# A constant tile written ahead of each row scatter on GpSimd, in place of a lag by tiles

## What is computed

```
x = x + cross_attention_0(layernorm(x), context 77 keys, 16 heads)
x = x + ffn_0(layernorm(x))          # top-1 gate of 8, LoRA of rank 4, relu
x = x + cross_attention_1(layernorm(x), context)
x = x + moe_1(layernorm(x))          # top-1 switch of 8 experts, 128 -> 512 -> 128, gelu
```

```
out[t] = x[t] + p[t] * (gelu(xn[t] @ w1[e] + b1[e]) @ w2[e] + b2[e])
```

## Time and profile before

| | us |
|---|---|
| three runs | 205.21, 207.39, 207.83 |
| their median | 207.39 |
| the profiled execution, its own time | 206.03 |
| its span in the profile | 204.2 |
| TensorE busy | 172.5 (84%) |
| VectorE busy | 124.7 (61%) |
| ScalarE busy | 90.5 (44%) |
| GpSimd busy | 59.9 (29%) |
| 22 output scatters on GpSimd, together | 21.6 |
| 8 row scatters on GpSimd, together | 8.4 |

### The profile page before, as it was taken

How to read it: one execution, slowest core, us unless ns; L and a number is a source line. 1 busy time by engine, 2 the same in 40 slices (tenths; PEclk the granted TensorE clock), 3 DMA queues, 4 the chain that set the end, 5 groups by cost and what they waited for, 6 DMA issues and landing times.

```text
span 204.2 us, 3819 instructions
## 1 busy us (share of the span) xinstructions
PE 172.5 (84%) x1168; PEld 141.8 (69%) x1169; DVE 124.7 (61%) x386; ACT 90.5 (44%) x216; POOL 59.9 (29%) x73
## 2 busy tenths in 40 slices
PE   7696899989999967698999998965988989989840
PEld 2435778979949944574886778853677979989730
DVE  2799967689733696983346976454477553644420
ACT  5490466245550443322248163331365556565520
POOL 8873030002205240100020002045006545655451
PEclk9997999999999997999999999997899999999995
DMA  5999990000000000000000000003801380100000
GB/s 203 279 322 404 464 400 11 0 0 3 2 0 3 0 0 0 2 3 0 0 0 3 0 0 0 3 28 100 263 9 52 98 246 25 31 5 9 24 17 2
DMA packets 9219, 15.37 MB, mean 75 GB/s; under 512 B 1578, under 2 KB 6069, under 8 KB 9136
## 3 DMA queue, kind: packets, MB, share of 16 engines
q1 hardware_dynamic: 7680, 13.00, 18.6%
q0 software_dynamic: 1088, 1.60, 2.4%
q10 hardware_dynamic: 432, 0.53, 0.7%
HBM read 13.53 MB, written 5.44 MB: 93 GB/s over the span
## 4 chain that ended last, share of the span: by engine, by line
PE 60%; DVE 23%; issue 5%; ACT 5%; DMA 2%; POOL 1%; ACTq 0%; DVEq 0%; another core or an unknown queue 0%; POOLq 0%
PE acc L1001 11%; PE scores L1104 10%; PE acc L1115 9%; DVE QG L721 4%; PE shared L1058 4%; PE shared L957 4%; PE scores L982 3%; PE shared L937 3%; PE shared L1044 3%; DVE MR L731 2%; DVE XN L680 2%; PE shared L909 2%; PE acc L886 2%; DVE stats L662 2%; PE shared L930 2%
## 5 line engine op out<-in xcount | busy, mean ns | idle before, releaser
L1001 PE MATMUL acc<-VP,P 123*128 123x128 f32 (+1 forms) x320 | 41.8, 276 | 0.6 <-ACT P L598 0.6
L1001 PEld LDWEIGHTS acc<-VP,P 123*128 123x128 f32 (+1 forms) x320 | 39.8, 191 | 2.8 <-ACT P L598 1.0
L598 ACT ACTIVATE P<-scores 123x512 f32<-123x512 f32 (+1 forms) x40 | 22.9, 595 | 26.4 <-PE scores L982 23.6
L638 ACT ACTIVATE HT<-scores,B 128x128 f32<-128x128 f32 x88 | 25.4, 376 | 11.7 <-PE scores L1104 5.7
L731 DVE TENSOR_REDUCE MR<-shared 128x4 f32<-128x308 f32 x64 | 26.9, 468 | 2.2 <-PE shared L957 2.0
L1104 PE MATMUL scores<-XST,HT 128*128 128x128 f32 x176 | 24.1, 280 | 3.7 <-ACT XST L631 3.3
L520 POOL DMA_INDIRECT out<-XS,token x22 | 21.6, 981 | 18.9 <-DVE XS L867 11.9
L506 POOL TENSOR_TENSOR X<-X,ROWS 128x512 f32<-128x512 f32 x6 | 7.6, 1274 | 65.7 <-DVE XN L680 65.6
L1104 PEld LDWEIGHTS scores<-XST,HT 128*128 128x128 f32 x176 | 21.4, 192 | 5.3 <-ACT XST L631 4.2
L1115 PE MATMUL acc<-W,HT 128*128 x176 | 23.2, 276 | 1.1 <-ACT HT L638 1.1
L957 PE MATMUL shared<-KG,QG 98*128 98x308 f32 x64 | 20.4, 378 | 4.3 <-DVE QG L721 3.4
(11 more groups left out here) (121 smaller groups left out, 248.9 us busy)
## 6 DMA issues: line engine op xcount, KB each, us to landing
W<-in_w SPq DMA_DIRECT2D x16, 256.0 KB, 7.9
slots<-in_empty SPq DMA_DIRECT2D x1, 2860.0 KB, 15.6
XS<-slots SPq DMA_DIRECT2D x2, 650.0 KB, 6.0
XS<-slots SPq DMA_DIRECT2D x2, 390.0 KB, 4.2
W<-in_ffn0w SPq DMA_DIRECT2D x1, 534.0 KB, 9.4
XS<-slots SPq DMA_DIRECT2D x2, 260.0 KB, 2.9
X<-in_x SPq DMA_DIRECT2D x2, 256.0 KB, 5.7
B<-in_b SPq DMA_DIRECT2D x1, 512.0 KB, 7.4
```

The costliest lines, as they stand in the source:

```text
L598: act.activation(P[0:w, n % NP], scores[n % 2][0:w, :], ACT.Exp).then_inc(probs_ready, 1)
L638: ins = act.activation(HG1[:, t % NHB, c], hidden[t % 2][:, c], ACT.Gelu_apprx_tanh, bias=B1[:, bass.ds(expert[t] * NF + k, 1)])
L1001: ins = pe.matmul(acc[qt // 2][:, c:c + VW], P[0:w, n % NP, 128 * qt:128 * qt + 128], VP[0:w, l, b, j, half], start=(t == 0 and qt % 2 == ...
```

## The change

GpSimd gets a tile `pause` of 128 partitions by 320 numbers, which nothing reads, and a function `rest`, which fills it with zeros and waits until that is done. `rest` is called ahead of each of the four row scatters of batch 1 and of each of the first 11 output scatters (t < NSB), 15 times in all. The table LAG goes: output scatter t now waits for tile t alone. The waits of the other engines, their instructions and their order stay as they are.

```diff
-LAG = [2] * 7 + [1] * 7 + [0] * (NS - 14)
...
+        pause = sb("pause", [128, 320])
...
+        rested = sem("rested")
...
             finish(pool.memset(mhalf[:, :], -0.5), powers)
+
+            def rest():
+                finish(pool.memset(pause[:, :], 0.0), rested)
+
             for s in steps:
...
                     for i in range(b * NQ, (b + 1) * NQ):
+                        if b == 1:
+                            rest()
                         pool.indirect_dma_start(slots, bass.IndirectOffsetOnAxis(ap=slot[:, i:i + 1], axis=0), ROW[:, i], None,
...
                     t = s[1] - 2
-                    pool.wait_ge(z_ready, t + 1 + LAG[t])
+                    if t < NSB:
+                        rest()
+                    pool.wait_ge(z_ready, t + 1)
```

## The result

The changed kernel took 208.34 us (median of four runs, 207.59 to 209.57) against 206.89 us for the kernel before (four runs, 205.21 to 207.83). The ratio is 1.016, with a 95% interval of 1.011 to 1.021. It is slower by more than its interval, and the forecast of 203.4 us had the sign wrong. The profiled execution took 207.80 us, against 206.03.

A forecast was written before the change was run, and what follows sets the result against it. TensorE was taken to set the pace of the 22 tiles, held up by late signals beside back-to-back scatters. From 206.03 us, 1.98 of TensorE idle time and 0.6 at the end came off: 203.4 us, range 200.4 to 208.6.

The forecast's parts named there:

- What bounds the kernel: Whole kernel: TensorE sets the pace of the 22 tiles; its 4.0 us of idle time are the most to win there.
- a period above 1.9 us: Sign of being wrong, scatters behind fills: they would fall behind for the rest of the kernel and end it later.
- The fills: GpSimd, 15 fills of 0.37 us: scatters come every 1.75 us, a gap of 0.78 us instead of 0.31.
- The end: Last output scatter: starts sooner behind its tile, at most 1.28 us to be had, 0.6 taken.
- Behind the last fill: From output scatter 11: GpSimd two to three tiles behind, some seven scatters back to back at 1.28 us, late signals return.
- TensorE's gain: TensorE between 157 and 182 us: all 1.98 us of idle time won, with bounds of 0 and 4.0.
- One long group: Rival, scatters from 154 to 190 us: gap too short, one unbroken chain with late signals, 209.2 us; chance 0.17.
- Nothing changes: Rival, TensorE: something beside the scatters makes signals late, so the fills do nothing, 206.0 us; chance 0.22.
- Everything evens out: Rival, to the kernel's end: each scatter stands alone, all 4.0 and 1.28 us go, 200.8 us; chance 0.23.
- The row scatters of batch 1: GpSimd before batch 1's loads: row scatters end 1.5 us later, which costs nothing because the loads have cover.
- the 2.6 us of cover: Batch 1's first tile: time left between its load landing and its transpose, even with TensorE 1.2 us earlier.
- one of the signs of being wrong: Batch 1's first transpose: T of tile 11 waiting for its load would show the forecast wrong.

The follow-up runs named there:

- E13: The kernel before, unchanged, run and profiled again on a fourth chip, without late signals: 200.52 us.
- E12: The changed kernel, unaltered, run again beside the kernel before on a fourth chip, without late signals: 206.66 us, ratio 1.030.
- E11: Against the kernel before: only the four fills ahead of the row scatters of batch 1, the table LAG kept: 200.76 us, ratio 1.003.

## Why the prediction was wrong

*What bounds the kernel.* Half right. TensorE's 4.0 us of idle time behind 157 us go with late signals, and where those are absent they are absent too (E13). But the kernel ends by its last scatter, which even there starts 1.5 us behind the last tile. The prediction priced GpSimd's queue as cover, and only in its last line ("a period above 1.9 us") as a bound.

*The fills: the step that failed.* "A gap of 0.78 us between scatters instead of 0.31", a period of 1.75 us between bounds of 1.65 and 1.86, measured 2.14 to 2.39. The fill's own 0.37 us was right (0.38). What was mis-sized is the start of the scatter behind it, taken as at most 0.21 us from the earlier trace rows: there a scatter starts at 197.89, 0.21 us after its tile. But that one stands 0.30 us behind another scatter, the bare gap, and the tile was no longer what it waited for. Behind a wait that ends last it is 0.79 us, and the trace of before showed that too, in the tile and the scatter that waits for it:

```profile
165.47 0.35 DVE L867 SCALAR_TENSOR_TENSOR XS<-acc,XS 128x128 f32<-128x128 f32 x1 [1.65 <-PE acc L1115]
...
166.61 0.97 POOL L520 DMA_INDIRECT out<-XS,token  x1 [2.14 <-DVE XS L867]
```

The tile ends at 165.82, and the scatter starts 0.79 us later. With 2.28 us for each of ten periods the eleventh output scatter stands at 184.75 instead of 179.4, and the last cannot start before 198.8, where the sum had it at 196.6. The term *The end* is part of this step: it took 0.6 us off for a last scatter that follows its tile, but by then GpSimd's queue decided when the last one starts.

*Behind the last fill.* "There the late signals come back, as they stand in the old trace": 2.0 us were kept, 8.16 were measured, since the chain was nine long instead of a few threes. The two are one error: GpSimd was seven tiles behind there, not two to three, since 18 were finished and 11 sent when the first scatter without a fill came.

*TensorE's gain.* Right in kind: 0.0 us idle between 155 and 187 us where the old trace had 1.98 between 157 and 182, with the gap at 1.2 us. It was worth nothing, since GpSimd's queue ended last. On a chip without late signals there is nothing to gain, and the change costs 3% (E12).

*The rivals.* None was the case. "One long group" had the sign and nearly the time (209.2 against 208.34), but that was luck, for through the fills nothing was late. "Nothing changes" came with the Trainium skill's rule (SBUF — State Buffer, Who interferes with whom) that TensorE and ScalarE wait for nobody. On four chips the traces agree with it: up to twelve close scatters and no held signal. On the fifth and in the first two traces something held TensorE's signals, and no page or run here names it. "Everything evens out" can't be judged by the change, whose last eleven scatters stood in a chain.

*The row scatters of batch 1.* Nothing in the time, but not with the 2.6 us of cover. The loads were issued at 163.59, 2.4 us later and not 1.5 (in E12 at 165.66, 4.4 later), and TensorE came to tile 11 at 165.68, 3.0 us earlier and not 1.2 (1.6 of it because this trace runs ahead). So its transpose waited for its load, one of the signs of being wrong. Its weight load shows the wait in the first trace of the change, and the transpose itself in E12:

```profile
165.68 0.14 PEld L1106 LDWEIGHTS shared<-CON,XS 128*128 128x128 f32 x1 [0.26 <-DMA XS<-slots]
```

```profile
167.84 0.33 PE L1106 MATMUL shared<-CON,XS 128*128 128x128 f32 x1 [0.35 <-DMA XS<-slots]
```

It cost nothing, since GpSimd's queue ended last, and E11, with the row fills alone, is level. In a kernel that TensorE ends, the cover would have been used up.

*Open.* Whether late signals go with a chip or with something that varies from one load of the program to the next: within each group the times of all runs and the traces say the same, and no chip came twice in the experiments. Whether spacing pays where they are is open as well. And a TensorE record's end is modelled, so the traces show that the product was taken up late, and not whether its signal was late or the product itself; "late signal" stands here for either.

## What to carry to other kernels

Before a pause is put in an in-order queue, add up that queue to the end: number left times the period, from where it starts. Here the slack was 0.6 us (1.28 against 1.9 for a tile), and a fill with the wait behind it cost 1.0. To size how an instruction starts behind a wait, take rows where that wait ended last, and not one that stands in a row of its own kind. And profile the kernel before on a second chip before explaining idle time that a change is meant to win.

## What the hardware showed unexpectedly

- An indirect DMA on GpSimd starts 0.30 us behind another one where nothing else holds it, but 0.77 to 0.87 us behind a fill that it waited for, in every trace with fills, and 0.79 us behind a tile that it waited for (166.61 in the first trace).
- TensorE's products were taken up as much as 8.5 us late during chains of scatters, in the first two traces and on one of the five chips, and in none of the 14 traces from the four others. The kernel before took 205.25 to 206.89 us where it happened and 199.58 to 200.53 where it didn't.
- The copy of W1 took 0.89 us beside the scatter of 164.26 and the fill behind it, against 0.43, and a fill 0.55 us beside a copy. The port rule of the Trainium skill (SBUF — State Buffer, Who interferes with whom) has such a copy and a GpSimd instruction block each other for the whole instruction. The trace of the change agrees only in part, since the copy of 155.69 took its 0.43 us inside the row scatter of 155.49, which lasted 0.97. TensorE never waited for a copy there.
